# Values of a head pair as one 128x64-tile matmul over a diagonal layout, with the scores in two parts around them

## What is computed

```python
B, F, E = (2048, 64, 128)
ATT_D, HEADS = (32, 4)
q = _split_heads(jnp.einsum('bfe,ed->bfd', x, W_query))
k = _split_heads(jnp.einsum('bfe,ed->bfd', x, W_key))
v = _split_heads(jnp.einsum('bfe,ed->bfd', x, W_value))
scores = jnp.einsum('hbqd,hbkd->hbqk', q, k)
attn = jax.nn.softmax(scores, axis=-1)
out = jnp.einsum('hbqk,hbkd->hbqd', attn, v)
out = out.transpose(1, 2, 0, 3).reshape(x.shape[0], x.shape[1], HEADS * ATT_D)
out = out + jnp.einsum('bfe,ed->bfd', x, W_res)
return jax.nn.relu(out)
```

## Time and profile before

| | |
|---|---|
| runs shown | 1584.31 us median of 3 (1581.49 to 1584.65) |
| the profiled execution | 1581.74 us, span of the instructions 1579.9 us |
| busy share of the span | PE 98%, PEld 91%, DVE 88%, ACT 69%, POOL 67% |
| DMA | 86 GB/s on the mean |

### The profile page before, as it was taken

How to read it: one execution, slowest core, us unless ns; L and a number is a source line. 1 busy time by engine, 2 the same in 40 slices (tenths; PEclk the granted TensorE clock), 3 DMA queues, 4 the chain that set the end, 5 groups by cost and what they waited for, 6 DMA issues and landing times.

```text
span 1579.9 us, 94069 instructions
## 1 busy us (share of the span) xinstructions
PE 1554.5 (98%) x40960; PEld 1442.6 (91%) x40960; DVE 1395.0 (88%) x1793; ACT 1095.7 (69%) x1794; POOL 1061.1 (67%) x1290
## 2 busy tenths in 40 slices
PE   6999999999999999999999999999999999999996
PEld 6899999999999999999999999999999999999996
DVE  5898989998989898988989898989898989889895
ACT  4677777676767676777767677767676767677774
POOL 2667676767666666666666767676666666666666
PEclk9999999999999999999999999999999999999999
DMA  3444444444444444444444444444444444444442
GB/s 61 86 90 85 89 85 88 87 87 87 87 86 87 89 86 91 83 91 84 90 84 90 85 88 87 87 87 87 87 87 88 86 90 85 91 83 90 84 89 56
DMA packets 677309, 135.45 MB, mean 86 GB/s; under 512 B 545888, under 2 KB 677216, under 8 KB 677216
## 3 DMA queue, kind: packets, MB, share of 16 engines
q1 hardware_dynamic: 675840, 134.30, 41.2%
q10 hardware_dynamic: 1376, 0.26, 0.1%
HBM read 67.37 MB, written 67.11 MB: 85 GB/s over the span
## 4 chain that ended last, share of the span: by engine, by line
PE 98%; issue 1%; POOL 0%; ACTq 0%; DMA 0%; DVE 0%; ACT 0%; POOLq 0%
PE ps_so L241 17%; PE ps_pt L230 16%; PE ps_so L219 14%; PE ps_qk L194 12%; PE ps_vr L207 8%; PE ps_qk L195 8%; PE ps_vr L208 8%; PE ps_qk L196 8%; PE ps_vr L209 8%; POOL y L156 0%; POOL y L162 0%; DMA w_raw<-in_L_rec_W_res_dram 0%; ACTq L330 0%; POOLq L41 0%; ACT qk L289 0%
## 5 line engine op out<-in xcount | busy, mean ns | idle before, releaser
L156 POOL TENSOR_TENSOR y<-attn,vr 128x256 f32<-128x256 f32 x512 | 389.2, 785 | 415.7 <-issue 409.3
L305 ACT COPY probs_t<-ps_pt 128x512 f32<-128x512 f32 x512 | 275.1, 590 | 317.7 <-PE ps_pt L230 317.7
L162 POOL TENSOR_SCALAR y<-y 128x512 f32<-128x512 f32 x256 | 461.1, 1801 | 22.4
L360 DVE TENSOR_REDUCE row_max<-ps_so 128x16 f32<-128x1024 f32 x256 | 313.6, 1225 | 132.1 <-PE ps_so L219 131.8
L289 ACT COPY qk<-ps_qk 128x512 f32<-128x512 f32 x512 | 301.2, 588 | 118.9 <-PE ps_qk L196 100.2
L194 PE MATMUL ps_qk<-x_hi,w_hi 128*128 128x256 f32 x1024 | 336.6, 329 | 11.0 <-DVE x_lo L351 9.5
L297 ACT COPY vr<-ps_vr 128x512 f32<-128x512 f32 x512 | 298.6, 583 | 33.2 <-PE ps_vr L209 1.2
L365 DVE TENSOR_TENSOR shifted<-ps_so,row_max 128x1024 f32<-128x1024 f32 x256 | 313.4, 1224 | 8.8
L207 PE MATMUL ps_vr<-w_hi,x_hi 128*128 128x256 f32 x1024 | 295.3, 288 | 1.2 <-ACT vr L297 0.7
L241 PEld LDWEIGHTS ps_so<-vr,probs_t 64*64 64x64 f32 x8192 | 262.2, 134 | 35.8 <-issue 1.6
L241 PE MATMUL ps_so<-vr,probs_t 64*64 64x33 f32 x8192 | 290.8, 221 | 1.4 <-POOL v_rows L171 1.4
(11 more groups left out here) (22 smaller groups left out, 2172.8 us busy)
## 6 DMA issues: line engine op xcount, KB each, us to landing
x_in<-in_r_x_dram SPq DMA_DIRECT2D x1024, 64.0 KB, 2.2
out_dram<-y SPq DMA_DIRECT2D x256, 256.0 KB, 2.3
w_raw<-in_L_rec_W_query_dram ACTq DMA_DIRECT2D x1, 64.0 KB, 2.2
w_raw<-in_L_rec_W_key_dram ACTq DMA_DIRECT2D x1, 64.0 KB, 2.6
w_raw<-in_L_rec_W_value_dram ACTq DMA_DIRECT2D x2, 32.0 KB, 2.6
w_raw<-in_L_rec_W_res_dram ACTq DMA_DIRECT2D x2, 32.0 KB, 2.5
```

What stands on the lines that cost most here:

```text
L156: nc.gpsimd.tensor_tensor(y[:, n % 2, a * HALF:(a + 1) * HALF].rearrange("k t (p j d) -> k j (t p) d", j=2, d=D), attn[:, n % 2, a * HALF: ...
L162: nc.gpsimd.tensor_scalar(y[:, n % 2], y[:, n % 2], 0.0, None, ALU.max).then_inc(y_ready, 1)
L360: nc.vector.reduce_max(row_max[:, :].rearrange("q (h u) -> q h u", h=HEADS), scores, AX_X).then_inc(max_ready, 1)
```

## The change

**Values.** A matmul now takes both heads of a pair at once. The stationary operand is the full 128 partitions of `probs_t` (keys of the first head below, of the second above) by the 64 queries of one sequence: two tiles of 128x64 in place of four of 64x64. The moving operand is a new buffer `v_diag` with 2 x 33 = 66 columns for each sequence and pair: the first head's values stand in the lower partitions of the first 33 columns, the second head's in the upper partitions of the last 33, and the rest is zero. There are 16 such matmuls a step in place of 32, with 66 moving columns in place of 33. `v_rows` is gone.

**POOL** zeroes the two `v_diag` buffers at the start (ahead of the identity's completion), and copies four blocks of 64 partitions by 8 x 33 a step in place of two of 64 by 264.

**Order on PE.** `score` is cut by halves. A step now is: scores of the first half, values of block i - 2, scores of the second half, transposes, projections. The last projection is whole again, and the waits stand ahead of what needs them.

**The rest.** The values' result of a tile now lies in bank u (33 columns for each of its four heads), so `inv_sum` and the product on DVE run over tile and head in another order. ACT's copy of `vr` no longer waits for `o_done`.

The diff, cut to its core:

```diff
-        v_rows = [sb(f"v_rows{n}", [P, 2, HALF, PAIRS, VW]) for n in range(2)]
+        v_diag = [sb(f"v_diag{n}", [P, SEQS, 2, HALF, PAIRS, 2, VW]) for n in range(2)]
...
-        inv_sum = sb("inv_sum", [P, HEADS, TILES])
+        inv_sum = sb("inv_sum", [P, TILES, HEADS])
...
                     for j in range(2):
-                        other = slice((1 - j) * F, (2 - j) * F)
-                        nc.gpsimd.tensor_copy(
-                            v_rows[n % 2][j * F:(j + 1) * F].rearrange("k a t p d -> k a (t p d)"),
-                            vr[n][other, :, j].rearrange("k a t p d -> k a (t p d)")).then_inc(v_moved, 1)
-                        pool.wait_ge(v_moved, i * 2 + j + 1)
+                        for m, seq in enumerate((1 - j, j)):
+                            nc.gpsimd.tensor_copy(
+                                v_diag[n % 2][j * F:(j + 1) * F, seq, :, :, :, j].rearrange("k a t p d -> k a (t p) d"),
+                                vr[n][seq * F:(seq + 1) * F, :, j].rearrange("k a t p d -> k a (t p) d"),
+                            ).then_inc(v_moved, 1)
+                            if m == 0 or j == 1:
+                                pool.wait_ge(v_moved, i * 4 + j * 2 + m + 1)
...
             last.then_inc(ones_ready, 1)
+            for n in range(2):
+                last = nc.gpsimd.memset(v_diag[n][:, :, :, :, :, :, :], 0.0)
+            last.then_inc(diag_zero, 1)
+            pool.wait_ge(diag_zero, 1)
...
-            def score(i):
-                for u in range(TILES):
+            def score(i, a):
+                for u in range(a * HALF, (a + 1) * HALF):
...
-            def weigh_values(i, n, a):
-                for t in range(HALF):
-                    for p in range(PAIRS):
-                        for j in range(2):
+            def weigh_values(i, n):
+                for a in range(2):
+                    for t in range(HALF):
+                        for p in range(PAIRS):
                             for s in range(SEQS):
-                                rows = slice(j * F, (j + 1) * F)
-                                at = (p * 2 + j) * BANK + O_AT + (a * HALF + t) * OW
-                                v = vr[n][rows, a, j, t, p, :] if s == j else v_rows[n % 2][rows, a, t, p, :]
+                                at = (a * HALF + t) * BANK + O_AT + p * 2 * VW
                                 last = nc.tensor.matmul(
-                                    ps_so[s * F:(s + 1) * F, at:at + VW],
-                                    probs_t[rows, a, t * PAIRS + p, s * F:(s + 1) * F],
-                                    v, start=True, stop=True)
-                return last
+                                    ps_so[s * F:(s + 1) * F, at:at + 2 * VW],
+                                    probs_t[:, a, t * PAIRS + p, s * F:(s + 1) * F],
+                                    v_diag[n % 2][:, s, a, t, p].rearrange("k j d -> k (j d)"), start=True, stop=True)
+                last.then_inc(o_done, 1)
 
             def step(i, n):
+                if has(i):
+                    if has(i - 1):
+                        pe.wait_ge(shifted_ready, i)
+                    if has(i - 3):
+                        pe.wait_ge(attn_ready, i - 2)
+                    pe.wait_ge(qk_ready, halves(i, 0))
+                    score(i, 0)
                 if has(i - 2):
-                    weigh_values(i - 2, (n + 2) % RING, 0)
-                    weigh_values(i - 2, (n + 2) % RING, 1).then_inc(o_done, 1)
+                    pe.wait_ge(pt_ready, halves(i - 2, 1))
+                    pe.wait_ge(v_moved, (i - 2) * 4 + 4)
+                    if not has(i):
+                        pe.wait_ge(shifted_ready, N)
+                        pe.wait_ge(attn_ready, i - 2)
+                    weigh_values(i - 2, n)
                 if has(i):
                     pe.wait_ge(qk_ready, halves(i, 1))
-                    score(i)
+                    score(i, 1).then_inc(s_done, 1)
...
                 if has(i):
-                    project_vr(i, n, 1, range(0, 1))
-
-                if has(i):
-                    pe.wait_ge(shifted_ready, i + 1)
-                if has(i - 2):
-                    pe.wait_ge(attn_ready, i - 1)
-                if has(i - 1):
-                    pe.wait_ge(pt_ready, halves(i - 1, 1))
-                    pe.wait_ge(v_moved, (i - 1) * 2 + 2)
-                if has(i):
-                    project_vr(i, n, 1, range(1, HALF))
+                    project_vr(i, n, 1)
...
-                    act.wait_ge(v_moved, i * 2 - 6)
-                    act.wait_ge(o_done, i - 3)
+                    act.wait_ge(v_moved, (i - 4) * 4 + 4)
...
-                heads = bank[:, :, O_AT:O_AT + TILES * OW].rearrange("q h (u d) -> q h u d", d=OW)
+                heads = bank[:, :, O_AT:O_AT + HEADS * VW].rearrange("q u (h d) -> q u h d", d=VW)
```

More of the change, by code:

```diff
@@ L24 @@
 VW = D + 1
-OW = D + 2
 O_AT = TILES * F
@@ L84, in attention_program @@
         ident_zero, ident_ready = sem("ident_zero"), sem("ident_ready")
-        ones_ready = sem("ones_ready")
+        ones_ready, diag_zero = sem("ones_ready"), sem("diag_zero")
         whi_ready, wlo_ready = sem("whi_ready"), sem("wlo_ready")
@@ L197, in project_qk, with project_vr @@
                 last.then_inc(qk_done, 1)
-            def project_vr(i, n, a, tiles=range(HALF)):
-                if tiles[0] == 0 and (a == 1 or has(i - 1)):
+            def project_vr(i, n, a):
+                if a == 1 or has(i - 1):
                     pe.wait_ge(vr_ready, halves(i, a) - 1)
@@ L203, in project_vr @@
                 w_vr_lo = w_lo[:, 2:4, :].rearrange("p w c -> p (w c)")
-                for t in tiles:
+                for t in range(HALF):
                     ps = ps_vr[:, t * 2 * COLS:(t + 1) * 2 * COLS]
@@ L209, in project_vr @@
                     last = nc.tensor.matmul(ps, x_lo[n][:, tok], w_vr_hi, start=False, stop=True)
-                if t == HALF - 1:
-                    last.then_inc(vr_done, 1)
-            def score(i):
-                for u in range(TILES):
+                last.then_inc(vr_done, 1)
+            def score(i, a):
+                for u in range(a * HALF, (a + 1) * HALF):
                     for s in range(SEQS):
                         for h in range(HEADS):
-                            a, b = u // HALF, u % HALF * SEQS + s
+                            b = u % HALF * SEQS + s
                             rows, at = slice(h * D, (h + 1) * D), h * BANK + u * F
@@ L221, in score @@
                                 qk[rows, a, 1, b * F:(b + 1) * F], start=True, stop=True)
-                last.then_inc(s_done, 1)
+                return last
             def transpose_probs(i, a):
@@ L375, in step @@
                     nc.vector.tensor_tensor(
-                        attn[:, n % 2].rearrange("q u h d -> q h u d"), heads[:, :, :, 0:D],
-                        inv_sum[:, :, :].unsqueeze(3).to_broadcast([P, HEADS, TILES, D]),
+                        attn[:, n % 2], heads[:, :, :, 0:D],
+                        inv_sum[:, :, :].unsqueeze(3).to_broadcast([P, TILES, HEADS, D]),
                         ALU.mult).then_inc(attn_ready, 1)
```

## The result

The changed kernel takes **1570.71 us** (median of 4 runs, 1570.47 to 1570.91); the kernel before took 1583.62 us beside it (median of 4). The ratio is **0.992**, with a 95% interval of 0.9903 to 0.9937: faster by 0.8%. I had forecast 1594 us, slower, so the sign was wrong; the time lies within the range. The span went from 1579.9 to 1568.7 us, by 11.2 us.

What follows compares the result with a forecast made beforehand. PE was taken as the bound, with 98% of the chain. Values +0.03, scores +0.04 and waits -0.035 gave +0.035 us a step, times 254 steps +9 us, plus 0.8 at the end: +10 us, median 1594 us, range 1545 to 1625.

Steps and rivals of the forecast that it cites:

- the scores in halves: Scores on PE: two runs of 0.29 us, each with a 0.15 us gap, 0.88 against 0.84 us: +0.04 us a step.
- the ends: Very end of the program: PE waits for POOL's copies, and two more copies make that 0.8 us longer, once.
- The waits: Last projection on PE: moving the wait for DVE's product removes a 0.14 us break in one step of four, -0.035 us a step.
- The values: Value matmuls on PE: 32 instructions at 30 ns and a 0.17 us gap, 1.10 against 1.07 us: +0.03 us a step.
- the faster rival: Scores and values on PE: gaps of 0.10 us, tiles keep 57 ns; -0.105 us a step, 1557 us; chance 0.35.
- POOL hidden, DVE and ACT untouched: Other engines: POOL needs 5.3 us of a 6.06 us step, copies at 403 ns stay hidden; DVE and ACT change nothing.
- The taking of turns: Value matmuls on PE: full-height tiles do not share the array, 57 ns an instruction, +0.925 us a step, 1819 us; chance 0.12.
- the signs by which I had wanted to know a wrong prediction: PE timeline: value pace over 36 ns, scores and values together under 1.8 or over 2.1 us, or the chain leaving PE.

## Why the prediction was wrong

**The sign.** The sum was +0.035 us a step; the middle steps show -0.022. Two terms failed, the scores in halves and the ends. Term by term:

- *The waits, -0.035.* Right, with its mechanism: -0.039 when moved alone. It was the largest gain of the change, near 10 us, and in my sum the two losses beside it outweighed it. Why the break came in one step of four is open (see above).
- *The values, +0.03.* Nearly right. The pace is 29.2 ns (I took 30), the block 1.08 to 1.09 us (1.10), the form alone +0.021. My reading that the moving columns do not set the pace holds at 66 columns, but by a margin of 2 ns in 58; that the weight load does is not shown by a run of its own.
- *The scores in halves, +0.04.* This is the term that decided the sign, and it failed. I took 0.29 us for a run of 32 and 0.15 for the gap behind it. The gap is 0.15 us, as I took it; the run is 0.27 us. A run with its gap is 0.42 (609.06 to 609.48), not 0.44, and twice that is just under the old 0.84. The 0.29 is the start of the 33rd score and stands in the trace of the kernel before too: both of my windows in the earlier trace rows already counted 33, and I took their end for the end of 32. The split measured by itself is -0.005 to -0.006. A mistake of 0.02 us, made twice, came to 11 us.
- *The ends, 0.8 us.* I looked for what the change adds there (the wait for the copies; the 0.9 us that the tail grew agrees with my 0.8), and not for what it removes. The long steps stood in the trace: two gaps of 0.91 and 1.15 us ended by "issue" among the last scores. I had read them as noise of the ending. The long steps at the two ends were worth 5 us, half of the result.

With -0.005 for the scores in place of +0.04, the sum for a step is -0.010, -2.4 us over the 238 middle steps; with -5.5 for the ends, -1.4 for the start and +0.9 for the tail it comes to -8.4, within 3 us of the measured -11.2. The rest is in the values, 0.01 a step less than I took, and the waits, 0.004 more. That the time lies in my range at all is owed to the faster rival, for which I had widened it.

**POOL hidden, DVE and ACT untouched:** right; 406 ns a copy, POOL busy 81% and nobody waits for it but at the very end.

**The rival that came nearest** was the faster one, with 1557 us and 0.35. It named the sign, and not the cause: it wanted gaps of 0.10 us beside the values, and they are 0.15 on either side. The taking of turns is refuted by the pace: a full-height tile gets an instruction each 58 ns. A weight load of 137 ns and a stream of 56 ns cannot follow each other within that. None of the signs by which I had wanted to know a wrong prediction came either (pace 29.2 ns, scores and values 1.92 us, the chain on PE): they watch a plain step, and the gain lay in the steps that are not plain. So the rule of the Trainium skill, "TensorE: Matmul & The Clock Gate", Part 3, The mechanism, that loads overlap with running matmuls only when the row group differs, does not hold for these tiles; the measurement decides. The same section names a background weight buffer as a second case in which a load is pulled ahead; whether that is at work here, no run shows.

**What stays open.** What makes PE 0.07 us late once in each pass of the loop, with DVE no later than in the other steps; which steps of written-out code become the long ones; and the second row maximum, which starts between 19.9 and 21.4 us from kernel to kernel without a pattern that I can name, and took 1.4 us of the 11.

## What to carry to other kernels

A semaphore wait in the middle of a dense run can cost though it is satisfied before its turn, and no row shows it as a wait: counted from the end of DVE's product, 0.10 us ahead cost 0.2 us in every step, 0.18 us ahead cost 0.14 us in one step of four, and 0.42 us ahead nothing. Compare single steps with each other, not only their mean, and look at the steps written out beside a loop. Where an engine's copy empties a bank that the next matmul but one needs, put other work of PE between the two uses until they are further apart than matmul, copy and semaphore together (0.96 us here): that was worth 3.5%, more than the whole change. And a term of a few hundredths of a microsecond that is the difference of two readings with that error must not decide a sign; counting in windows of 0.01 us, the old trace would have given the 0.27 us.

## What the runs showed that I had not expected

- On a 64-column tile, each of the two PE instructions of a 32-bit matmul takes 57 ns with 33 moving columns (64x64 tile), 58 with 66, and 112 with 132 (128x64 tile): up to 66 the moving columns cost nothing, at 132 they cost 0.85 ns each.
- A loop body of eight steps (some 2600 matmuls and loads) ran at 1840 us and one of four at 1581: with eight, the instruction queue brought 6.19 MB, with four 0.25. Somewhere between the two sizes the code is no longer kept from pass to pass. Behind the stops the granted clock was at 0.50, and that lengthened a further step of each pass.
- Written out without a loop, the same 40960 matmuls took 1779 us, and the 32768 of the changed kernel 1629: with so many instructions to a microsecond, PE waits for code that is not in a loop.
- The same wait is worth 10 us in the kernel before, moved by two matmuls, and 53 us in the changed one, moved by three.
- A change of tile shape around the values costs 0.15 us from the last start to the first, whatever the length of the run behind it.
